# Expert products by halves of the tokens, token weights multiplied in ahead of the down product, and all engines' calls written out in another order

## What is computed

```python
x = x + attn(_layernorm(x), w_qkv, ln_w, w_proj)          # groups of 32 tokens, 16 heads of 8
x = x + xattn(_layernorm(x), ctx_1024, ...)               # 16 heads of 64, 64 context rows
# the experts, on h = _layernorm(x):
scores  = sigmoid(h @ router_w.T)                         # 1024 x 16
combine = top-4 of 16 inside the 2 best of 4 groups, by score + bias; weights normed, times 2.5
h_e = h @ gate_w[e];  u_e = h @ up_w[e]                   # 128 x 128 each
y_e = (silu(h_e) * u_e) @ down_w[e]
routed = sum over e of y_e * combine[:, e]
x = x + routed + (silu(h @ sh_gate) * (h @ sh_up)) @ sh_down
```

## Time and profile before

| | |
|---|---|
| median of 3 runs | 221.75 us (221.56 to 221.85) |
| the profiled execution's span | 220.4 us |
| TensorE busy / VectorE / ScalarE / GpSimd | 87% / 71% / 44% / 40% of the span |
| mean granted TensorE clock | 0.985 |

### The profile page before, as it was taken

The page is one execution under the profiler, slowest core; times in us unless marked ns, Lnnn a source line. Parts: engine busy times, 40 slices in busy tenths (PEclk is TensorE's granted clock), DMA queues, the critical chain, the costliest instruction groups (busy, mean ns, idle before and its releaser), DMA issues.

```text
span 220.4 us, 5287 instructions
## 1 busy us (share of the span) xinstructions
PE 192.7 (87%) x1803; PEld 153.7 (70%) x1803; DVE 155.9 (71%) x410; ACT 96.3 (44%) x235; POOL 88.3 (40%) x174
## 2 busy tenths in 40 slices
PE   6788599777969998999997957899999999999991
PEld 5565466545646675777786836778888888888890
DVE  3665435665445686488889779999787878878883
ACT  2456576867774457455555452122222322223220
POOL 5476436444551975366655232223322243220000
PEclk9969889999999999999999999999999999999999
DMA  4987000000000110000000000100001000000003
GB/s 93 325 223 222 3 3 4 3 3 0 3 0 3 52 48 0 0 3 0 1 3 0 0 0 24 28 25 27 25 28 43 24 24 0 0 0 0 1 3 95
DMA packets 10952, 7.39 MB, mean 34 GB/s; under 512 B 1697, under 2 KB 10162, under 8 KB 10802
## 3 DMA queue, kind: packets, MB, share of 16 engines
q1 hardware_dynamic: 10930, 7.10, 11.1%
HBM read 6.57 MB, written 0.52 MB: 32 GB/s over the span
## 4 chain that ended last, share of the span: by engine, by line
PE 58%; ACT 12%; DVE 11%; POOL 10%; issue 5%; DMA 1%; SPq 0%; DVEq 0%; ACTq 0%; POOLq 0%
PE bank L1306 12%; PE wide L1140 7%; PE bank L1169 6%; POOL kbd L446 3%; PE wide L1191 3%; PE wide L1194 3%; PE wide L1192 3%; PE wide L1195 3%; PE wide L1196 3%; PE wide L1193 3%; PE bank L1154 2%; ACT k L589 2%; ACT v L589 2%; DVE act L968 2%; PE bank L1110 2%
## 5 line engine op out<-in xcount | busy, mean ns | idle before, releaser
L694 ACT ACTIVATE sil<-wide 128x512 f32<-128x512 f32 x36 | 21.4, 597 | 60.1 <-PE wide L1193 60.0
L984 DVE SCALAR_TENSOR_TENSOR x<-bank,combine,x 128x128 f32<-128x128 f32 x128 | 35.9, 345 | 8.9 <-PE bank L1306 8.1
L1306 PEld LDWEIGHTS bank<-dn_w,act 128*128 128x128 f32 x256 | 33.2, 191 | 2.5
L1306 PE MATMUL bank<-dn_w,act 128*128 (+1 forms) x256 | 33.4, 275 | 0.0
L469 POOL TENSOR_TENSOR gu_hi<-gu_w,zero_col 128x256 fp32r<-128x256 f32 x18 | 11.0, 613 | 47.4 <-PE wide L1196 47.4
L968 DVE TENSOR_TENSOR act<-sil,wide 128x512 f32<-128x512 f32 x36 | 24.7, 687 | 4.2 <-ACT sil L694 1.3
L446 POOL TENSOR_TENSOR kbd<-qkT,hmask 128x512 f32<-128x512 f32 x8 | 11.2, 1395 | 23.6 <-ACT qkT L552 23.6
L1191 PE MATMUL wide<-x3hi,gu_lo 128*128 128x512 f32 x36 | 17.3, 479 | 3.3 <-DVE act L968 2.8
L1169 PE MATMUL bank<-vo_fold,p2T 128*128 128x128 f32 x128 | 17.6, 282 | 0.0
L1169 PEld LDWEIGHTS bank<-vo_fold,p2T 128*128 128x128 f32 x128 | 15.7, 192 | 1.0
L1140 PE MATMUL wide<-qk_fold,xn2T 128*128 128x512 f32 x32 | 15.3, 601 | 0.6 <-ACT qk_fold L593 0.4
(11 more groups left out here) (154 smaller groups left out, 408.8 us busy)
## 6 DMA issues: line engine op xcount, KB each, us to landing
wkv_sb<-in_L_xattn_w_kv_dram SPq DMA_DIRECT2D x1, 1024.0 KB, 6.2
gu_w<-in_L_ffn_gate_w_dram SPq DMA_DIRECT2D x16, 64.0 KB, 1.8
gu_w<-in_L_ffn_up_w_dram SPq DMA_DIRECT2D x16, 64.0 KB, 2.0
x<-in_x_dram SPq DMA_DIRECT2D x8, 64.0 KB, 4.2
wq_sb<-in_L_xattn_w_q_dram SPq DMA_DIRECT2D x1, 512.0 KB, 4.2
wout_sb<-in_L_xattn_w_out_dram SPq DMA_DIRECT2D x1, 512.0 KB, 4.6
out_dram<-x SPq DMA_DIRECT2D x8, 64.0 KB, 1.6
wqkv_sb<-in_L_attn_w_qkv_dram SPq DMA_DIRECT2D x1, 192.0 KB, 2.3
```

The source lines that it names most:

```text
L694: sc.activation(sil[:, j % 2, :], bank[j % 2], ACT.Silu).then_inc(sil_s, 1)
L984: dve.scalar_tensor_tensor(out=x[:, t, :], in0=bank[4 + (j + 2) % 4][:, m * D:(m + 1) * D], scalar=combine[:, t, bass.ds(e, 1)], in1=x[:, ...
L1306: last = pe.matmul(bank[4 + (j + 2) % 4][:, m * D:(m + 1) * D], act[:, j % 4, m * P:(m + 1) * P], dn_w[:, bass.ds(n, 1), :].rearrange("p o ...
```

## The change

- Experts: the 36 units now run k = 18 c + n, all 18 experts for the first 512 tokens, then for the others. `gate_up` is split into `gate` and `up` (three products each), which stand apart in the order. `up_bank` keeps the four banks of `wide` in two pairs.
- Down: `down` is one product of 128x512 with the down weights as the stationary tensor and the activations as the moving one; its result is features by tokens. All 18 of a half are summed in one PSUM bank (FOLD for the first half, PV for the second). At the end of each half ScalarE copies the bank (`copy_y`), TensorE turns it by four transposes (`turn_y`), and VectorE adds it to x once (`add_y`). The 128 scalar_tensor_tensor are gone.
- Token weights: `transpose_rows` turns combine of a half to rows, `copy_rows` and `store_rows` bring them to DRAM, and 32 loads (`load_spread`), each of 4 rows to all 128 partitions (256 KB), bring them back into four buffers that lie in wkv_sb. GpSimd multiplies (`weigh`, 32 times, 128x512) into three buffers aw, from which `down` reads.
- Expert weights: no ring. All of gu_hi and gu_lo are kept, the raw gate and up weights are loaded in 8 transfers over v2, once the last fold unit is done, and the down weights in two over wq_sb and wqT, once the last A is. Eleven tiles share memory with tiles of the attention.
- Cross-attention: for tiles 4 to 7 `scores2` uses one pair of banks, `transpose_p2` one bank for both halves (PT2[1]); the last `norm_p2` is GpSimd's as well.
- Routing: by halves of four tiles, with fewer instructions. x and the output are moved by fewer, larger transfers; wq is loaded earlier, and wkv after all of x.
- The loops over steps and units are replaced by a written list of calls on every engine.

```diff
-    RING = 4
+    SPREAD = 4
+    LOADS = 4
...
+        spread = wkv_sb[:, :].rearrange("p (s t q) -> p s t q", s=SPREAD, t=TPC)
+        sil = kbd[:, :, :, :, :].rearrange("p n g h k -> p n (g h k)")
+        act = [s1[:, n, :, :].rearrange("p h k -> p (h k)") for n in range(2)] + [p1[:, n, :] for n in range(2)]
+        aw = [vbd[:, n, :, :, :, :].rearrange("p g r h d -> p (g r h d)")[:, 0:CHUNK] for n in range(3)]
...
+            def load_spread(k):
+
+                c, e = k // NE, k % NE - NSH
+                r = loads_before(k)
+                if e == 0:
+                    sp.wait_ge(rows_st, 16 * (c + 1))
+                if r < SPREAD:
+                    sp.wait_ge(f_copied, unit_no[("kv", NPAIR - 1)] + 1)
+                else:
+                    used = [n for n in range(k) if routed(n)][r - SPREAD]
+                    sp.wait_ge(*weighted(used))
+                sp.dma_start(spread[:, r % SPREAD, :, :],
+                             w_rows[c].rearrange("(t e) q -> e t q", e=E)[e].partition_broadcast(P)
+                             ).then_inc(sp_l[r % SPREAD], 16)
...
+            def weigh(k):
+
+                r = loads_before(k)
+                pool.wait_ge(g_s, k + 1)
+                pool.wait_ge(sp_l[r % SPREAD], 16 * (r // SPREAD + 1))
+                if k >= 3:
+                    pool.wait_ge(y_s, k - 2)
+                pool.tensor_tensor(aw[k % 3], act[k % 4],
+                                   spread[:, r % SPREAD, :, :].rearrange("p t q -> p (t q)"), ALU.mult).then_inc(awp_s, 1)
...
+            def down(k):
+
+                c, n = k // NE, k % NE
...
+                if routed(k):
+                    if k == NSH:
+                        pe.wait_ge(dn_l, 48)
+                    pe.wait_ge(*weighted(k))
+                    rhs = aw[k % 3]
+                else:
+                    pe.wait_ge(g_s, k + 1)
+                    rhs = act[k % 4]
+                pe.matmul((FOLD, PV)[c], dn_of(n), rhs, start=(n == 0), stop=(n == NE - 1)).then_inc(y_s, 1)
+
+            def turn_y(c):
+
+                pe.wait_ge(yc_s, c + 1)
+                pe.wait_ge(*((res2_s, NT) if c == 0 else (fin_s, 1)))
+                for m in range(TPC):
+                    last = pe.transpose(QK[:, m * D:(m + 1) * D], y_sb[:, m * P:(m + 1) * P], ident[:, :])
+                last.then_inc(yt_s, 1)
```

More of the change, by code:

```diff
@@ L308, in decoder_layer, with routed, weighted, loads_before @@
-        units = [u for i in sorted(units_at) for u in units_at[i]]
-        unit_no = {u: n for n, u in enumerate(units)}
-        STEPS = 2 * NT + 4
+        ONE_PAIR = 4
+        BY_VECTOR = ()
+        def routed(k):
+            return NE * (k // NE) + NSH <= k
+        def weighted(k):
+            same = [n for n in range(k + 1) if routed(n) and (n in BY_VECTOR) == (k in BY_VECTOR)]
+            return (awv_s if k in BY_VECTOR else awp_s), len(same)
+        def loads_before(k):
+            return sum(routed(n) for n in range(k))
@@ L517, in _ @@
+            weigh(26)
+            weigh(27)
+            weigh(28)
+            weigh(29)
+            weigh(30)
+            weigh(31)
+            weigh(32)
+            weigh(33)
+            weigh(34)
+            weigh(35)
         @block.scalar
@@ L1001, in _ @@
[L1001 to L1009 removed]
+            norm_stats(0, 2)
@@ L1317, in _ @@
[L1317 to L1325 removed]
+            fold(("ctx", 0))
@@ new lines, in _ @@
+            output2(7, 0)
+            transpose_xn(2, 5, T1[:, P:2 * P])
+            output2(7, 1)
+            logits(5)
+            up(2)
+            transpose_xn(2, 6, T1[:, P:2 * P])
+            down(0)
+            logits(6)
+            gate(3)
+            transpose_xn(2, 7, T1[:, P:2 * P])
+            gate(4)
+            logits(7)
+            down(1)
+            up(3)
+            transpose_rows(0)
+            up(4)
+            gate(5)
+            gate(6)
+            up(5)
@@ new lines, in _ @@
+            gate(7)
+            up(6)
+            gate(8)
+            up(7)
+            gate(9)
+            down(2)
+            down(3)
+            down(4)
+            up(8)
+            up(9)
+            down(5)
+            gate(10)
+            up(10)
+            up(11)
+            down(6)
+            gate(11)
+            down(7)
+            gate(12)
+            gate(13)
+            up(12)
+            up(13)
+            down(8)
+            gate(14)
+            down(9)
+            gate(15)
@@ new lines, in _ @@
+            down(10)
+            gate(16)
+            up(14)
+            up(15)
+            down(11)
+            up(16)
+            transpose_rows(1)
+            down(12)
+            gate(17)
+            down(13)
+            up(17)
+            gate(18)
+            down(14)
+            gate(19)
+            down(15)
+            up(18)
+            up(19)
+            gate(20)
+            up(20)
+            down(16)
+            gate(21)
+            up(21)
+            down(17)
+            up(22)
@@ new lines, in _ @@
+            down(18)
+            up(23)
+            gate(22)
+            down(19)
+            gate(23)
+            up(24)
+            gate(24)
+            turn_y(0)
+            up(25)
+            down(20)
+            down(21)
+            gate(25)
+            up(26)
+            down(22)
+            gate(26)
+            gate(27)
+            down(23)
+            gate(28)
+            up(27)
+            gate(29)
+            gate(30)
+            up(28)
+            down(24)
+            up(29)
```

1387 lines of the change are left out of this document (933 added, 454 removed).

## The result

The changed kernel takes 237.72 us (median of four runs, 237.24 to 239.58) beside 221.72 us for the kernel before: a ratio of 1.073, 95% interval 1.069 to 1.078. The prediction said 205, between 196.5 and 213, so it missed the sign and the range. The profiled execution spans 235.3 us against 220.4.

What follows compares the result with a forecast made beforehand. The prediction took the order of the calls, not an engine, to bound self-attention. Its terms, 78.0 + 37.0 + 81.9 + 1.5 + 5.1, gave a span of 203.5 us; with 1.35 for the median, 205, range 196.5 to 213.

Steps and rivals of the forecast that it cites:

- The load, 3 us: Expert part: one spread load of token weights, 512 packets of 512 bytes, was taken to last 3 us.
- rival 5: Expert part: spread loads set the pace from 7.4 us each; at 10 us, 226 in total, slower than before; chance 0.07.
- 1.5 us of stall: Before the first routed downs: TensorE waits 1.5 us for weighed activations; 0 with a quick store, 5 if a hop doubles.
- rival 2: GpSimd bounds cross-attention, total 210, or first routed downs wait 5 us for their weights, 208.5; together chance 0.15.
- For the second half all this has a long lead: Second half of the expert part: the token weights' way through store, loads and weighs was said to start well ahead.
- Stretch A: Start to the first p2 transposes: 78.0 us against 85.5 before, with self-attention rounds of 6.2; bounds 73 and 85.
- Rival 1: Start to the first p2 transposes: this stretch doesn't shorten and takes 85 us, total 212; chance 0.12.
- Stretch B: First to last p2 transposes: 37.0 us, 33.6 of TensorE work and 3.4 of idleness, against 36.6 before; bounds 34 and 42.
- Stretch C: Last p2 transposes to the last down: 81.9 us of TensorE work, against 93.4 before.
- Rival 4: Expert units: products step at 0.215 us instead of 0.232, 3.7 us less, total 201; chance 0.04.
- the tail, 5.1: After the last down: copy, transposes, addition and store take 5.1 us, against 4.9 before.
- Rival 6: Newly dense start: lower granted clock eats the gain, total 207 with twice the earlier cost; no separate chance given.

Runs made afterwards that it cites:

- e2: The changed kernel with spread loads reading gate weight matrices, each packet from its own address, so the output lacks the token weights; 212.32 us.
- e3: The changed kernel with an expert's four weight rows side by side in DRAM, one 2 KB run per partition; 212.04 us, 0.958 of before.
- e4: The changed kernel with only the store of the first half's output moved behind the last spread load on SP; 229.32 us, 1.038 of before.
- e8: The changed kernel with both e3's row layout and e4's store order; 212.82 us.
- e1: The changed kernel with the 32 spread loads left out, weighs kept, so the sum lacks the token weights; 211.24 us, 0.953 of before.
- e14: The kernel of e8 run again on another chip as a control; 212.08 us, 0.955 of before.
- e13: e8 with products 14 and 15 ahead of the second routing's last two parts, and combine weights turned three downs later; 209.87 us, 0.941 of before.
- e11: The changed kernel with 68 idle 128-column products on TensorE ahead of the first three routed downs; 238.49 us.
- e5: e3's row order with 32 unused bytes after each row, so rows lie 544 bytes apart and loads are 512 packets again; 214.78 us.
- e9: The changed kernel's row order with 32 unused bytes after each row, so an expert's rows lie 8,704 bytes apart, not 8,192; 220.7 us.
- e7: The changed kernel with one spread buffer in place of four and the output store last on SP; 430.76 us in a single run.
- e6: The changed kernel with eight spread buffers in place of four; 224.5 us, 1.005 of before.

## Why the prediction was wrong, step by step

*The load, 3 us.* This is the step that failed. I took it from down_w (2,048 packets in 6.0 us; the row prints 0.5 KB, the count follows from the tensor's shape) and wq, rows whose every packet has an address of its own. For such a source the figure was right (2.9 in e2). For w_rows, with four addresses 8,192 bytes apart and each read 128 times, it was 8.1 in the median and 7.8 for the very first. The prediction named the difference, in rival 5 ("each load reads the same four rows for all 128 partitions"), and then answered it with the very row that doesn't have it. Before, only two small loads are read by all partitions, each with other loads beside it:

```profile
rowb<-in_L_ffn_bias_dram SPq DMA_DIRECT2D x1, 8.0 KB, 4.8
rowb<-in_L_xattn_gate_dram SPq DMA_DIRECT2D x1, 0.5 KB, 5.0
```

They say little of 256 KB, but they don't support 3 us either. It was a guess from the wrong kind of row, and it entered the sum and the range without an upper bound of its own.

*Rival 5, chance 0.07.* The mechanism and its threshold of 7.4 us were right: at 8.1 it decides. Its price was not: (8.1 + 1.3 + 0.2)/4 is 2.40 a unit, 5 us over 32 units, where the loss beside e3 was 26. It counted only the steady pace. Left out was the start: the first load alone takes 7.8, which makes the first way of the weights 10.4 us (combine turned at 124.1, weigh at 134.5) and not 5.5, and the three issued right behind it land 11.4 to 11.8 after their issue (up to 13.1 at 196.8). That is the step "1.5 us of stall; 0 if the store is quick, 5 if a hop costs twice as much", and TensorE waited 5.1 us before the first and 1.8 before the second routed down, so the second half of rival 2 came true with it. Left out were also the same again at the start of the second half, and GpSimd's splits, which stand in order behind weighs that wait, so that TensorE waits for gu_lo too (2.5 us). Of the first sixteen loads, which went out over 37.4 us, four need some 3 (as at 177.0) and the twelve that reuse a buffer 34, about 2.9 a unit.

*"For the second half all this has a long lead."* Wrong: only four loads have it. The fifth stood behind store_out(0) on SP. e4 prices that at 8 us with slow loads, e8 beside e3 at nothing with quick ones. I had listed what stood on SP ahead of the rows, but not what stood between the loads, nor what the store itself waits for.

*Stretch A, 78.0.* Right: 77.4, with rounds of 6.2 (said 6.2), the last qkT at 56.5 (56.3). The start was 13.2, not 12.3, and the seven rounds took 43.3 us (43.4) with nothing to be seen of the 0.6 for one more copy of A: part of how well 56.5 fits is luck, since these two misses nearly cancel. Nor is 77.4 firm, as the same calls end between 76.0 and 80.7 in the other profiled executions. Rival 1 is out all the same.

*Stretch B, 37.0.* Right: 36.8, and 36.8 again in e1, e3 and e14. GpSimd was busy 30.6 of 36.5 there and held nobody up, so the first half of rival 2 is out. Whether the 37.0 was rightly made up of 33.6 of work and 3.4 of idleness can't be read off: TensorE's records fill 35.84 of 36.50 us, but they overlap. (Before, the stretch is 37.3 by the same first and last transpose, 85.5 to 122.8; rows 2 cut it at 122.1.)

*Stretch C, 81.9, and the stall of 1.5.* Its counts and steps hold: e3 has the 68 products behind the last p2 transposes, and units of 2.25 us. What the term lacked is VectorE. In e3 TensorE waits 1.5 us for combine weights, 1.5 for a product and 1.2 for weighs; the sentence "VectorE now has 0.69 a unit besides routing" left out that routing steps take up to 1.3 us beside the weighs that the same change puts on GpSimd. From the last p2 transposes to the end of the span the prediction has 88.5 us; e14 has 95.0 (112.8 to 207.8), e13 92.8 (114.7 to 207.5). So with quick loads the sum was 4 to 6.5 us short, and even without loads (e1) 5.9 short of the sum less its stall. The named waits are 4.2 of that in e3; the rest was not taken apart. The forecast of 205 would therefore have been missed by some 7 us with a landing of 3 us as well, only on the right side of before and inside the range.

*Rival 4, products at 0.215.* Out: five of six still step by 0.23.

*Weigh, 1.4 (1.27), the store of the rows, 1.6 (1.8), the tail, 5.1.* All near enough; together under half a microsecond.

*Rival 6, the clock.* The mean granted clock fell to 0.937 (0.985 before), but not for the dense start: there it was lower once, near 15 us, where before had it twice; the rest lies behind the waits from 134 us on. In the one stretch that e11 filled, that cost little.

## What to carry to other kernels

A DMA's duration is a matter of its addresses as much as of its bytes and packets: take it only from a row that reads the same way, and where there is none, give it an upper bound and follow that bound through. If many partitions read the same rows, lay those rows side by side, so that each partition's read is one packet (8.1 to 3.2 us here, for the price of an output pattern on VectorE). And when a view gives one median for many transfers, look at one that goes out alone too: here 8.1 and 7.8, but 5.8 and 3.5. Price a slow hop in three places and not one: the first use, each refill, and what stands in order behind the one who waits, on SP and on GpSimd too. And work moved to GpSimd is not free for VectorE, even where neither waits for the other's data.

## What the runs showed of the hardware

- 512 packets of 512 bytes, issued as one DMA from DRAM, median of the 32 loads of a kernel: 2.9 us with an address for each (e2); with four addresses for all 128 partitions 4.0 (544 bytes apart, e5), 5.8 (8,704 apart, e9) and 8.1 (8,192 apart, the changed kernel). As 128 packets of 2 KB from one address: 3.2 (e3).
- The same with no other load under way (the first of each kernel): 2.8 us (e2), 4.1 (e5), 3.5 (e9), 7.8 (the changed kernel) and 3.2 (e3).
- The slow load is slow in a kernel that never has two under way as well (e7: 7.7 us, 34 GB/s). With up to six under way (e6) they took 10.6 us, one landed every 2.1 us, and the instruction that issues one lasted up to 4.22 us instead of 0.36.
- A VectorE step of 128x64 elements took 0.22 us, and up to 1.32 where a GpSimd instruction on 128x512 elements ran at the same time.
